# Four weight buffers and 71 blocks in the expert stages of a four-layer gated cross-attention kernel

## The reference: what is computed

```python
x = x + tanh(g_xattn[l]) * attention_l(layernorm(x), ctx)
x = x + tanh(g_ffn[l]) * ffn_l(layernorm(x))
```

```python
# layer 0 (gate_up_w: 8 x 768 x 128, down_w: 8 x 128 x 384), plus one shared expert
top_v, top_i = top_k(softmax(normed @ router_w.T), 2)
comb = sum(one_hot(top_i) * softmax(top_v))
out = sum_e comb[:, e] * (silu(gate_e) * up_e) @ down_w[e].T + shared(normed)
# layer 3 (w1: 8 x 512 x 128, w2: 8 x 128 x 512)
out = sum_e cw[:, e] * (gelu(x @ w1[e].T + b1[e]) @ w2[e].T + b2[e])
```

## Time and profile before

| | |
|---|---|
| median of 3 runs | 3023.58 us |
| the profiled execution: span from first to last instruction | 2951.3 us |
| mean granted TensorE clock over the span | 0.923 |
| busy share: PE, DVE, ACT, POOL | 82%, 55%, 47%, 33% |
| all DMAs | 220.06 MB, mean 75 GB/s |
| weight loads of the experts | 144, landing 3.8 us after issue in the median |
| experts of layer 0 | about 588 to 915 us |
| experts of layer 3 | about 2578 to 2912 us |

### The profile page before, as it was taken

The page is one execution under the profiler, slowest core; times in us unless marked ns, Lnnn a source line. Parts: engine busy times, 40 slices in busy tenths (PEclk is TensorE's granted clock), DMA queues, the critical chain, the costliest instruction groups (busy, mean ns, idle before and its releaser), DMA issues. The chain is left out here.

```text
span 2951.3 us, 72710 instructions
## 1 busy us (share of the span) xinstructions
PE 2427.0 (82%) x27302; PEld 1747.2 (59%) x27302; DVE 1636.3 (55%) x4333; ACT 1385.7 (47%) x2082; POOL 983.8 (33%) x1065
## 2 busy tenths in 40 slices
PE   4788785699996899989999987999788887088882
PEld 2455553488884555567777764666455555077872
DVE  3789997444443677722222215888668888133332
ACT  2555553233332566645454544666456664044441
POOL 4446775534442222100000000111212555544444
PEclk8999986899997999989999998999789998599996
DMA  3111111256663222100000001111111111256667
GB/s 106 23 23 39 43 42 33 83 170 195 200 190 118 66 57 57 36 5 0 0 0 0 0 13 40 42 42 42 38 30 29 50 53 52 85 177 196 190 191 227
DMA packets 143811, 220.06 MB, mean 75 GB/s; under 512 B 27178, under 2 KB 94514, under 8 KB 143027
## 3 DMA queue, kind: packets, MB, share of 16 engines
q1 hardware_dynamic: 96930, 90.25, 12.1%
q10 hardware_dynamic: 29232, 90.37, 9.7%
q0 software_dynamic: 17408, 36.21, 3.5%
HBM read 157.48 MB, written 43.61 MB: 68 GB/s over the span
## 5 line engine op out<-in xcount | busy, mean ns | idle before, releaser
L679 POOL DMA_INDIRECT yg<-ysb,yidx x288 | 280.0, 972 | 415.7 <-DVE ysb L2133 184.3
L1673 DVE TENSOR_REDUCE mx<-psS 128x16 f32<-128x1024 f32 x264 | 322.0, 1220 | 153.9 <-PE psS L1199 152.7
L791 ACT ACTIVATE work<-psT 128x1024 f32<-128x1024 f32 x260 | 265.9, 1023 | 246.1 <-PE psT L1208 243.8
L785 ACT ACTIVATE work<-work 128x1024 f32<-128x1024 f32 x264 | 278.2, 1054 | 148.9 <-DVE work L1675 143.6
L1199 PE MATMUL psS<-kexp,qT 64*64 64x512 f32 x2112 | 293.9, 627 | 58.0 <-DMA kexp<-kT 46.7
L1675 DVE TENSOR_TENSOR work<-psS,mx 128x1024 f32<-128x1024 f32 x264 | 323.2, 1224 | 9.0
L478 POOL TENSOR_TENSOR ve<-mv,eps 128x4 f32<-128x4 f32 x85 | 17.2, 203 | 922.5 <-DVE mv L1649 922.0
L1208 PEld LDWEIGHTS psT<-ident,work 128*128 128x128 f32 x2080 | 242.5, 147 | 126.1 <-issue 66.3
L1208 PE MATMUL psT<-ident,work 128*128 128x128 f32 x2080 | 291.8, 286 | 2.9 <-ACT work L791 2.4
L1532 PEld LDWEIGHTS psY<-w_ffn,work 128*128 128x128 f32 x2016 | 247.6, 192 | 9.3 <-DVE work L2104 1.2
L1532 PE MATMUL psY<-w_ffn,work 128*128 128x128 f32 x2016 | 248.4, 275 | 1.6 <-DVE ysb L2127 1.0
(11 more groups left out here) (265 smaller groups left out, 4658.6 us busy)
## 6 DMA issues: line engine op xcount, KB each, us to landing
w_ffn<-in_wmoe ACTq DMA_DIRECT2D x72, 578.0 KB, 3.9
w_ffn<-in_wmoe ACTq DMA_DIRECT2D x72, 576.0 KB, 3.8
ctxT<-in_ctxT SPq DMA_DIRECT2D x76, 256.0 KB, 2.7
xin<-xg SPq DMA_DIRECT2D x144, 132.0 KB, 2.7
kexp<-kT SPq DMA_DIRECT2D x1152, 16.0 KB
gio<-yg SPq DMA_DIRECT2D x16, 512.0 KB, 4.2
work<-yg SPq DMA_DIRECT2D x16, 512.0 KB, 6.4
yg<-ysb,yidx POOLq DMA_INDIRECT x288, 3.2
```

The lines of the kernel that those rows point to most:

```text
L679: e.indirect_dma_start(out=yg, out_offset=bass.IndirectOffsetOnAxis(ap=yidx[:, b, t:t + 1], axis=0), in_=ysb[:, b, t, :], in_offset=None, ...
L785: e.activation(sc[:, s % 2], sc[:, s % 2], ACT.Exp).then_inc(p_ok, 1)
L791: e.activation(pT[:, s % 2, :], psT[:, :], ACT.Copy).then_inc(pt_ok, 1)
L1673: e.tensor_reduce(mx[:, :], src, AX, ALU.max).then_inc(s_max, 1)
```

## The change

WBUF is split into RBUF = 3 (rows, indices, gates and results) and WBUF = 4 (weights). The weight buffers now take the first 4624 columns of w_ffn, and the third ring place gets 1056 columns of its own behind them, so the wait for sd2 before a load falls away. ACT issues four loads at the start, and in the loop load j+3 instead of j+2, behind the same waits. The weight semaphores are no longer one set per layer but four for both, so their counts go on from layer 0 to layer 3 (wl_count). NB is 71 instead of 72: 16384 routed rows in blocks of 256 with 8 experts fill at most 64 + 7 blocks. The last waits of results_out count blocks per buffer, as 71 is no multiple of 3.

```diff
-NB = 2 * TOK // SLOT + E
+NB = 2 * TOK // SLOT + E - 1
-WBUF = 3
+RBUF = 3
+WBUF = 4
-        w_ffn = sb("w_ffn", [P, 4096])
+        w_ffn = sb("w_ffn", [P, WBUF * 1156 + GT * XW])
-        ring = [gio[:, 0, :, :], gio[:, 1, :, :], w_ffn[:, 4096 - GT * XW:4096].rearrange("p (t d) -> p t d", d=XW)]
+        ring = [gio[:, 0, :, :], gio[:, 1, :, :], w_ffn[:, WBUF * 1156:].rearrange("p (t d) -> p t d", d=XW)]
-        xin = sb("xin", [P, WBUF, 2, XW])
+        xin = sb("xin", [P, RBUF, 2, XW])
...
+        wl = [sem(f"wl{k}") for k in range(WBUF)]
...
+        def wl_count(lay, j):
+
+            return 16 * (lay // 3 * len(range(j % WBUF, NB, WBUF)) + j // WBUF + 1)
...
                 def rows_in(j):
-                    b = j % WBUF
-                    if j >= WBUF:
-                        sp.wait_ge(m["t_ps"], j - WBUF + 1)
-                        sp.wait_ge(m["row"], 4 * (j - WBUF + 1))
+                    b = j % RBUF
+                    if j >= RBUF:
+                        sp.wait_ge(m["t_ps"], j - RBUF + 1)
+                        sp.wait_ge(m["row"], 4 * (j - RBUF + 1))
...
-                for b in range(WBUF):
-                    e.wait_ge(m[f"ys{b}"], 32 * (NB // WBUF))
+                for b in range(RBUF):
+                    e.wait_ge(m[f"ys{b}"], 32 * ((NB - b + RBUF - 1) // RBUF))
...
                 e.wait_ge(m["tab"], 1)
                 for j in range(WBUF):
-                    if j == 2:
-                        e.wait_ge(m["sd2"], 16 * 2 * GT * (NG // 4))
                     weights_in(j)
...
-                        if 1 <= j < NB - 2:
-                            weights_in(j + 2)
+                        if 1 <= j < NB - WBUF + 1:
+                            weights_in(j + WBUF - 1)
```

More of the change, by code:

```diff
@@ L151, in program @@
         yfin = [work[:, b * 2 * CW:(b + 1) * 2 * CW].rearrange("p (t c d) -> p t c d", t=LT, c=2) for b in range(4)]
-        xin = sb("xin", [P, WBUF, 2, XW])
-        yidx = sb("yidx", [P, WBUF, 2], I32)
+        xin = sb("xin", [P, RBUF, 2, XW])
+        yidx = sb("yidx", [P, RBUF, 2], I32)
         yflag = sb("yflag", [P, 2, 2, 2])
-        ygate = sb("ygate", [P, WBUF, 2])
+        ygate = sb("ygate", [P, RBUF, 2])
         eb = sb("eb", [P, 2, NB])
         tokc = sb("tokc", [P, TILES])
-        ysb = sb("ysb", [P, WBUF, 2, D])
+        ysb = sb("ysb", [P, RBUF, 2, D])
         xgT = sb("xgT", [P, 2, SLOT])
@@ L217, in program @@
                 "row", "y2", "c_ok", "lg", "rk") + (("b_ok",) if n == 3 else ())}
-            for k in range(WBUF):
+            for k in range(RBUF):
                 MO[n][f"xl{k}"] = sem(f"m_xl{k}_{n}")
-                MO[n][f"wl{k}"] = sem(f"m_wl{k}_{n}")
                 MO[n][f"ys{k}"] = sem(f"m_ys{k}_{n}")
@@ L1067, in weights_in @@
                     row = e.value_load(table[0:1, j, 1:2], min_val=0, max_val=(E - 1) * P)
-                    e.dma_start(wg[:, b, 0:WROW[lay]], a[f"wmoe{lay}"][bass.ds(row, P), :]).then_inc(m[f"wl{b}"], 16)
+                    e.dma_start(wg[:, b, 0:WROW[lay]], a[f"wmoe{lay}"][bass.ds(row, P), :]).then_inc(wl[b], 16)
                 e.wait_ge(m["tab"], 1)
                 for j in range(WBUF):
-                    if j == 2:
-                        e.wait_ge(m["sd2"], 16 * 2 * GT * (NG // 4))
                     weights_in(j)
@@ L1084, in experts @@
                         e.activation(msg[:, b, :], psB[b][0][:, 0:n * SLOT], ACT.Silu).then_inc(m["act_ok"], 1)
-                        if 1 <= j < NB - 2:
-                            weights_in(j + 2)
+                        if 1 <= j < NB - WBUF + 1:
+                            weights_in(j + WBUF - 1)
                     else:
-                        e.wait_ge(m["wl%d" % (j % WBUF)], 16 * (j // WBUF + 1))
+                        e.wait_ge(wl[j % WBUF], wl_count(lay, j))
                         if j >= 2:
@@ L1491, in turn_x @@
                 def turn_x(j):
-                    b = j % WBUF
-                    e.wait_ge(m[f"xl{b}"], 16 * (j // WBUF + 1))
+                    b = j % RBUF
+                    e.wait_ge(m[f"xl{b}"], 16 * (j // RBUF + 1))
                     if j >= 1:
@@ L2107, in rows @@
                 def rows(j):
-                    b = j % WBUF
+                    b = j % RBUF
                     flag, part = yflag[:, j % 2, 0, :], yflag[:, j % 2, 1, :]
-                    e.wait_ge(m[f"xl{b}"], 16 * (j // WBUF + 1))
-                    if j >= WBUF:
-                        e.wait_ge(m[f"ys{b}"], 32 * (j // WBUF))
+                    e.wait_ge(m[f"xl{b}"], 16 * (j // RBUF + 1))
+                    if j >= RBUF:
+                        e.wait_ge(m[f"ys{b}"], 32 * (j // RBUF))
                     e.tensor_tensor(flag, xin[:, b, :, D], eb[:, 1, j:j + 1].broadcast_to([P, 2]), ALU.is_equal).then_inc(m["row"], 1)
@@ L2120, in result @@
                 def result(j):
-                    b = j % WBUF
+                    b, wb = j % RBUF, j % WBUF
                     e.wait_ge(m["dn_ps"], j + 1)
@@ L2128, in result @@
                     else:
-                        e.wait_ge(m["wl%d" % b], 16 * (j // WBUF + 1))
-                        e.tensor_tensor(ysb[:, b, :, :], y, wg[:, b, 1028:1156].rearrange(
+                        e.wait_ge(wl[wb], wl_count(lay, j))
+                        e.tensor_tensor(ysb[:, b, :, :], y, wg[:, wb, 1028:1156].rearrange(
                             "p (a d) -> p a d", a=1).broadcast_to([P, 2, D]), ALU.add).then_inc(m["b_ok"], 1)
```

## The result

The changed kernel takes 2956.91 us, the median of 4 runs (2956.32 to 2963.93), beside 3023.55 us for the kernel before (4 runs, 3021.88 to 3025.56): a ratio of 0.978, with the interval 0.977 to 0.980. It is 66.6 us faster, where 65.4 were forecast. In the profile of after the lines have moved: turn_x is L1500, the up of layer 3 L1522, the down product L1535, the weight load L1073, the row fetch L418, the scatter L684, the first pass of the rows L2116, the results L2130 to L2136.

A forecast was written before the change was run, and what follows sets the result against it. PE bounds the kernel, stopped in the expert stages by late weight loads. Savings of 20.5 us in layer 0 and 44.9 in layer 3, together 65.4, take 3023.6 to 2958.2 us, range 2941 to 2986.

The forecast's parts named there:

- The load's lateness: Expert weight loads: 1.3 us late in layer 3, 0.3 in layer 0; one period more lead ends the wait entirely.
- The next limit: Three-buffer loop of rows and results: no slack at 3.73 us in layer 3; spread makes it 3.90, layer 0 4.20.
- S: Row loop, 4P >= 8.53 + S + X: time until a scatter lands, taken as the median 3.4 us.
- X: Row loop, 4P >= 8.53 + S + X: time until a row fetch lands, taken as the median 3.0 us.
- DVE's order: On DVE rows(j+1) stands in front of result(j), a second coupling; by itself it costs nothing.
- DMA load: Layer 3 transfers rise to 221 GB/s, share 0.73; fetches run 2.8 us behind a load, so X isn't raised.
- Rival B: Row loop replaces the weights' waits: S and X grow 0.6 us each, both periods 4.25, total 2985 us; chance 0.17.
- rival D: Loads hold back rows and results; slower from S + X = 10.3 us in layer 3, 3087 at 11.0; chance 0.03.
- The block: Expert stages: one block less in each saves 4.20 + 3.90 = 8.1 us on PE's path.
- The start: Start of expert stages: dropped sd2 wait and fourth load cost zero, at most 1.4 us a stage.
- the 72.3 us around the span: Difference of measured median 3023.6 and profiled span 2951.3, taken as untouched and added to the forecast span 2885.9.
- Rival A: Both expert stages at PE's own pace, 4.15 and 3.73 us: 80.4 us saved, 2943.2 us; chance 0.2.

The follow-up runs named there:

- e4_no_lead: Changed kernel with four weight buffers and 71 blocks, but three loads at the start and load j+2 issued behind the old waits: 2950.44 us, ratio 0.996.
- e2_wbuf4_only: Changed kernel with 72 blocks instead of 71, so the four weight buffers alone: 2960.33 us, ratio 0.979.
- e8_after: The changed kernel itself, unedited, run again on the second chip: 2891.24 us, ratio 0.976.
- e7_rows4: Changed kernel with four buffers for rows and still three for results, third chip: 2882.96 us, ratio 0.973.
- e11_results4_again: Changed kernel with four buffers for results, indices and gates and three for rows, repeated on the third chip: 2879.61 us, ratio 0.972.
- e5_half_lead: Changed kernel with three loads at the start and load j+2 issued right behind activation j, not waiting for down(j-1): 2909.89 us, ratio 0.983.
- e1_71_only: Kernel before with 71 blocks instead of 72, still three weight buffers: 3012.10 us, ratio 0.996.
- e0_before: Kernel before, without an edit, profiled once more on the first chip: 3025.62 us, ratio 1.000.
- e9_both4: Changed kernel with four buffers for rows and four for results, second chip: 2877.17 us, ratio 0.972.
- e6_results4: Changed kernel with four buffers for results, indices and gates and three for rows, first chip: 2938.45 us, ratio 0.972.
- e10_half_both4: Changed kernel with four row and four result buffers, but load j+2 issued right behind activation j, third chip: 2881.80 us, ratio 0.973.

## Why the prediction was right, and where it was not

**The load's lateness: right.** It was put at 1.3 us in layer 3 and 0.3 in layer 0, against one period more of lead. The waits went from 29.1 and 5.9 us to none. e4_no_lead shows that the lead alone does this.

**The next limit: right in place and size, the size partly by luck.** The loop result, scatter, row pass, fetch was said to just fit with 3.73, and to cost 3.90 with the spread. Measured are a quiet pace of 3.73 and means of 3.89 (after) and 3.97 (e2_wbuf4_only, e8_after). Its waits are 4.5 us in after, or 6.3 with those that have no releaser, 9.2 in e8_after and 11.1 in e2_wbuf4_only, for 5 to 15 forecast. A fourth buffer on either side of the loop brings 3.73 to 3.77. But the working had the loop tighter than it is. S was taken as 3.4 us, the median of all scatters; the second scatter of a block, which the row pass waits for, lands after 3.1 us in the mean of layer 3, in before and after alike. X was taken as 3.0 and is 2.5 in e8_after. So 8.53 + 3.1 + 2.5 is 14.1 us where four periods of 3.73 are 14.9: a usual round has 0.8 us in hand (1.15 measured in front of turn_x), not none. The late turns aren't every second round by 0.7 us either, but seven to nine of 71 or 72, and much of their time (2.1 of 6.3 us in after, 7.6 of 9.2 in e8_after, 6.7 of 11.1 in e2_wbuf4_only) is in one to three fetches of 4 to 6 us. The 0.17 for the spread was an estimate with a halving in it, and two other executions of the same loop gave 0.24. In layer 0 4.20 was forecast, 4.18 and 4.19 measured.

**DVE's order costs nothing: nearly right.** e7_rows4 leaves it as it is and PE's waits for rows are 0. It has 2.6 us of waits for results in layer 3 (after 1.6, e11_results4_again 0.6), so this coupling costs about 2 us at most there.

**DMA load: right for this kernel, for a reason that the prediction gave only for the fetch.** S and X didn't grow: the row pass comes 3.0 to 3.3 us behind the second scatter, as in the profile of before (3.1 and 3.2), and the median of the fetches' landings in e8_after is 2.6 us in layer 0 (2.5 in layer 3). The prediction had looked at the phase between a fetch and the load ahead of it, 2.8 us, which is about what after shows (2.5 in the median of layer 3). It had not looked at the load behind the fetch, and had taken S as a length of its own. e5_half_lead shows that the time from the second scatter to the row pass is 3.0 to 3.3 or 4.1 to 4.4 us depending on where the load goes out. The changed kernel issues each load at the place where the kernel before did, so S didn't move. Rival B (both landings 0.6 us longer) is the mechanism of e5_half_lead, with other sizes: there the row pass comes 0.9 to 1.5 us later and the median fetch lands after 3.0 to 3.1 us, and the periods are 4.35 and 4.04, where B had 4.25 and 4.25. The bound of rival D was worked out wrongly: by the loop's own formula layer 3 passes today's 4.49 from S + X = 4 x 4.49 - 8.53 = 9.4 us, not from 10.3, and the two longest landings sum to 9.7. No run came near it.

**The block: right within its error, which is wide.** 8.1 us forecast; e1_71_only gives 12.7 (8 to 18) where a block is 4.4 us and two are 8.9, e4_no_lead 11 (7 to 15).

**The start: right.** e4_no_lead leaves out the wait for sd2 and has its gain in the two blocks alone. A fourth load at the start can't be seen: PE's first wait in layer 3 is 70.3 us in after, 70.1 in e4_no_lead.

**A step that failed without hurting the sum: "the 72.3 us around the span are not touched".** Only 1.9 us lie around the span of after (2955.0 in a run of 2956.87), 1.8 around that of e0_before. The 72 us were inside, in the shared expert and the attention stages, most likely because the profile and the times of before come from chips that differ by 2%. The sum was not hurt, for the difference lies in stages that the change doesn't touch, and the expert stages differ by 1.7 and 3.7 us. The number should have been doubted: no row of the profile of before supported 72 us ahead of its first or behind its last instruction. The sum could have failed had the change touched the shared expert.

**The sum.** Layer 0 saved 20.8 us for 20.5 forecast and layer 3 44.9 for 44.9, both profiles taken as they are; 66.6 measured for 65.4. Agreement to 0.3 us a stage is luck: on the first chip, against e0_before, after saves 22.5 and 48.6 us, and e8_after against the profile of before saves 19.8 and 40.8. Rival A's 80.4 us are what the four-buffer forms reach: 83.4 (e9_both4), 86.8 (e6_results4) and 82.4 (e11_results4_again).

## What to carry to other kernels

Count how late a transfer is as its landing time less the lead from issue to use; one buffer more gives one period more of lead, and then the next ring of the same loop can be the limit, so write down its periods and landings as well, the longest beside the median (here a usual round had about 1 us in hand, a few long fetches broke through it, and one more buffer there was worth another 14 us). When a transfer's issue is moved, look at what small DMAs go out close to it and whether a short ring waits for their completion. And see that the profile and the times are of one chip: their difference should be the few us around the span.

## What the runs showed of the hardware

**A small DMA's landing depends on a large one's issue.** A block's second scatter (128 rows) lands 2.8 us after its issue in e9_both4 and 4.2 us after it in e10_half_both4 (means, layer 0), and inside the loop the two differ only in where a load of 576 KB is issued. The data packets themselves are late: the last one ends 2.4 and 3.8 us after the issue, and the last update of the semaphore follows 0.4 and 0.5 us behind it.

**Chips differ in the routed stages and the shared expert.** The kernel before takes 3025 us on one chip and 2961 to 2962 on two others. Between the two profiled spans of it there are 73 us. Attention 0 has 9 of them, attention 3 has 15, and the shared expert is 53.0 us longer, of which some 10 come back in a shorter wait for the first rows. From the end of experts 0 to the end of attention 2, 1201 us, the two agree within 0.5 us. POOL issues 48 scatters in the shared expert, one each 1.28 us on both chips. In e0_before and in after, DVE, ACT and PE stand still for long times meanwhile. Two instructions of after, layer 0, start of the shared expert, with the idle time before them:

```profile
561.59 0.75 DVE L2041 SCALAR_TENSOR_TENSOR x_sb<-psY,tg,x_sb 128x512 f32<-128x512 f32 x1 [19.70 <-issue]
...
573.02 1.09 PE L1460 MATMUL psX<-ident,aT 128*128 128x128 f32 x4 [29.75 <-issue]
```

and the same multiplication in the profile of before, which has no idle time in front of it:

```profile
551.08 0.74 DVE L2038 SCALAR_TENSOR_TENSOR x_sb<-psY,tg,x_sb 128x512 f32<-128x512 f32 x1
```

The long stops are 7 to 31 us and most have no releaser in the profile ("issue"). What stops these engines, and why on one chip only, stays open, and so does what lengthens attention 3; no run was made for it.
